# A state-space and attention kernel with a hand-written slot table: the projection of u, its copy and the softplus take earlier slots

## What is computed

```python
# layer 1
xn = layernorm(x) * (1 + scale) + shift               # from silu(c) @ ada_w
x_in, z = split(xn @ in_proj_w.T)                     # 512 channels each
u = silu(causal_conv4(x_in) + conv_b)
dt_r, B, C = split(u @ x_proj_w.T, [64, 80])          # 64 + 16 + 16 rows: "x_dbl"
dt = softplus(dt_r @ dt_proj_w.T + dt_proj_b)
h[t] = h[t-1] * exp(dt * A) + (dt * u) * B            # 512 channels x 16 states
y = (sum_n h * C + u * D) * silu(z)
x = x + gate * (y @ out_proj_w.T)
# layer 2
q, k, v = projections of layernorm(x); q = softmax over head, k = softmax over positions
y = q @ (k.T @ v);  x = x + silu(layernorm(y) * (1 + s) + t) @ W_out + b_out
```

## Time and profile before

| | us |
|---|---|
| median of 3 runs (lowest, highest) | 557.86 (556.59, 559.77) |
| the profiled execution, its own time | 559.76 |
| its span in the trace | 558.0 |
| VectorE busy | 504.7 |
| POOL, PE and ScalarE busy | 449.6, 438.2 and 430.8 |
| VectorE idle ahead of scans, for ScalarE's decays | 10.9 in 14 waits |

### The profile page before, as it was taken

How to read it: one execution, slowest core, us unless ns; L and a number is a source line. 1 busy time by engine, 2 the same in 40 slices (tenths; PEclk the granted TensorE clock), 3 DMA queues, 4 the chain that set the end, 5 groups by cost and what they waited for, 6 DMA issues and landing times. The chain is left out here.

```text
span 558.0 us, 7398 instructions
## 1 busy us (share of the span) xinstructions
PE 438.2 (79%) x2438; PEld 364.5 (65%) x2438; DVE 504.7 (90%) x520; ACT 430.8 (77%) x992; POOL 449.6 (81%) x306
## 2 busy tenths in 40 slices
PE   8968756769688788779788678769677878959797
PEld 7657445557576677657676667658565766847675
DVE  2489899999999989999999999999999988999853
ACT  2694868689879989798979989799877797686444
POOL 4059979989997989979997999979997979995121
PEclk8978868887899698998899899989899697779899
DMA  8295043102330144011430044003320044000001
GB/s 250 90 330 150 0 140 97 68 23 77 120 114 2 28 153 170 3 28 52 152 122 0 29 156 168 0 11 117 122 85 9 2 165 159 1 0 20 1 1 38
DMA packets 22366, 45.38 MB, mean 81 GB/s; under 512 B 3684, under 2 KB 13556, under 8 KB 22328
## 3 DMA queue, kind: packets, MB, share of 16 engines
q1 hardware_dynamic: 22328, 44.92, 24.6%
HBM read 42.52 MB, written 2.39 MB: 80 GB/s over the span
## 5 line engine op out<-in xcount | busy, mean ns | idle before, releaser
L545 POOL TENSOR_TENSOR hs<-dtu,Br 128x1024 f32<-128x1024 f32 x127 | 296.8, 2360 | 7.9 <-DMA Br<-bc_rows 6.9
L766 ACT ACTIVATE ring<-dt,Aneg 128x256 f32<-128x256 f32 x512 | 212.7, 464 | 44.0 <-DVE hs L1012 39.1
L1000 DVE TENSOR_TENSOR_SCAN ring<-ring,hs 128x1024 f32<-128x1024 f32 x97 | 221.6, 2284 | 10.9 <-ACT ring L766 10.9
L1370 PE MATMUL sums<-ident,hs 128*128 128x128 f32 x1024 | 154.9, 309 | 49.4 <-DVE hs L1012 49.3
L1370 PEld LDWEIGHTS sums<-ident,hs 128*128 128x128 f32 x1024 | 138.6, 162 | 60.6 <-DVE hs L1012 57.5
L1012 DVE TENSOR_TENSOR hs<-ring,Cr 128x1024 f32<-128x1024 f32 x96 | 117.5, 1224 | 3.3
L554 POOL TENSOR_TENSOR hs<-hs,Cr 128x1024 f32<-128x1024 f32 x31 | 73.0, 2356 | 38.7 <-DVE hs L1000 38.7
L1000 DVE TENSOR_TENSOR_SCAN hs<-ring,hs 128x1024 f32<-128x1024 f32 x31 | 70.3, 2268 | 0.0
L1437 PE MATMUL PY<-wqkvo,xT 128*128 128x256 f32 x168 | 48.3, 439 | 0.0
L1437 PEld LDWEIGHTS PY<-wqkvo,xT 128*128 128x128 f32 x168 | 39.6, 236 | 7.7
L1363 PE MATMUL sums<-ident,uD 128*128 128x128 f32 x64 | 14.3, 310 | 32.3 <-DVE ygT L1019 32.3
(11 more groups left out here) (232 smaller groups left out, 681.7 us busy)
## 6 DMA issues: line engine op xcount, KB each, us to landing
Br<-bc_rows SPq DMA_DIRECT2D x32, 512.0 KB, 5.3
Cr<-bc_rows SPq DMA_DIRECT2D x32, 512.0 KB, 4.0
xg<-in_x SPq DMA_DIRECT2D x8, 256.0 KB, 3.0
out<-fin SPq DMA_DIRECT2D x7, 256.0 KB, 4.3
hs<-in_ada_wT SPq DMA_DIRECT2D x3, 512.0 KB, 5.1
win<-in_in_wT SPq DMA_DIRECT2D x2, 512.0 KB, 6.9
hs<-in_W_emb SPq DMA_DIRECT2D x2, 512.0 KB
gate<-gate_rows SPq DMA_DIRECT2D x8, 128.0 KB, 3.1
```

Source lines behind the costliest of these rows:

```text
L545: nc.gpsimd.tensor_tensor(hs[:, g % DBUF], dtu[:, b % 2, dc, :].unsqueeze(1).to_broadcast([P, NQ, T]), Br[:, NQ * q:NQ * q + NQ, :], ALU.m ...
L766: ins = nc.scalar.activation(ring[:, g % 2, j, :], dt[:, b % 2, dc, :], ACT.Exp, scale=Aneg[:, c:c + 1])
L1000: V.tensor_tensor_scan(driven if by_pool(g) else decays, decays, driven, 0.0, ALU.mult, ALU.add).then_inc(s_scan_done, 1)
L1370: ins = M(YT[:, c, :], hs[:, g % DBUF, j, P * c:P * c + P], ident[:, :], is_transpose=True, start=False, stop=(q == UPC - 1 and j == NQ - ...
```

## The change

On TensorE `x_proj` goes from slot -9 behind `output` to slot -10 ahead of it, and `dt_proj_0` from slot -8 to -9. On ScalarE `copy_xdbl` goes from slot -6 to -8, `softplus_parts_0` from -5 to -6, `softplus_parts_1` from -3 to -4, and `norm1`, which keeps slot 26, now stands ahead of `softplus_parts_0` in the table. Entry 0 keeps its old place by an extra line. Slots -6 and 26 and 42 are all position 10.

```diff
                 for slot, step in (..., (-14, conv_last_tap_1),
-                                   (-11, copy_z), (-6, copy_xdbl), (-5, softplus_parts_0), (-3, softplus_parts_1),
-                                   (19, copy_yg), (25, normalize1), (26, norm1), (30, exp_q), (30, exp_k), (31, mask_v), (32, copy_qT),
+                                   (-11, copy_z), (-8, copy_xdbl), (26, norm1), (-6, softplus_parts_0), (-4, softplus_parts_1),
+                                   (19, copy_yg), (25, normalize1), (30, exp_q), (30, exp_k), (31, mask_v), (32, copy_qT),
                                    (33, copy_kT), (36, normalize2), (42, finish), (-29, moments0)):
...
+                    if step is softplus_parts_0 and g in (-6, -5):
+                        b = 0 if g == -5 else None
...
-                                   (-13, in_proj_3), (39, output), (-9, x_proj), (-8, dt_proj_0), (-6, dt_proj_1),
+                                   (-13, in_proj_3), (-10, x_proj), (39, output), (-9, dt_proj_0), (-6, dt_proj_1),
```

## The result

The changed kernel takes 569.86 us (median of 4 runs, 569.21 to 570.15), the kernel before beside it 557.25 us (4 runs, 556.59 to 559.77): a ratio of 1.0216, 95% interval 1.0181 to 1.0251. The forecast was 566.3 us, with a range of 561.8 to 573.0. Two profiles can be compared term by term: 569.21 us and a span of 567.4 after, 559.76 and 558.0 before, so 9.4 us between the spans. The rest of the 12.6 us between the medians lies between each profiled execution and its median: before, the median was 2.5 us lower, after, 0.65 us higher. In the ratios of this document runs over 1.5% above the fastest of their own kernel are left out, though not in the medians: one in "The softplus put back" and three in "x_proj alone".

A forecast was written before the change was run, and what follows sets the result against it. VectorE, 90% busy, was taken to bound the kernel, so only its idle time could change. Window losses of +5.0 and TensorE lateness of 3.4 gave +8.4 us on the 557.86 median: 566.3 us, range 561.8 to 573.0.

The forecast's parts named there:

- The bound: VectorE, 90% busy with an unchanged instruction list, bounds the kernel; the change can act only on its idle time.
- The window: ScalarE, position 10's decays to position 11's scan: 5.85 us available, 5.36 needed before the change, 7.39 after.
- The forecast's 1.54 us a window: Excess of ScalarE's work over the window, waited for by VectorE in units 43, 59, 75, 91 and 107.
- the forecast's 5.0: First sum for position 11: 7.70 us in five windows plus 1.06 in unit 27, less 3.79 of waits removed.
- TensorE's lateness: Moved x_proj delays ScalarE at TensorE's lower clock: 0.85 us in each of four entries, 3.4 in all.
- The 3.0 us through `transpose_x1` and `norm1`: In unit 43's entry at half clock, transpose_x1 ends up to 3.0 us after norm1 wants it.
- The upper bound of +15.4: TensorE lateness of 3.0 us in three entries and 1.4 in unit 27, on top of 5.0.
- What was costed at nothing: Zero cost for softplus_parts_1 between decays of positions 12 and 13, later finish, earlier broadcasts and later sums of position 7.
- a sign of being wrong: VectorE beginning to wait in a position held for covered: 8, 12 or 13.
- Its other terms at nothing: Zero taken for unit 11's decays (bounds 0 and 0.5 us) and, within the upper bound, position 8's gating product.
- The rival of a slow TensorE: TensorE stays as slow as in the profile before: +15.4 us, 573.3 us; chance 0.17.
- a TensorE fast everywhere: Filling the gap raises the clock before x_proj in all entries, only the window counts: +5.0, 562.9 us; chance 0.25.

The follow-up runs named there:

- The softplus put back: Changed kernel with both softplus halves back in slots -5 and -3, its other moves kept: 562.18 us, ratio 1.0045 to the kernel before.
- x_proj alone: Kernel before with only x_proj moved from slot -9 to -10, ahead of the sums of position 7 and output: 558.74 us, ratio 0.9978.
- the second profile: Profile of the changed kernel timed once more, unedited, beside the kernel before: 569.05 us, ratio 1.0181.

## Why the forecast was right, and where it was not

**The bound.** Right: VectorE's instruction list is unchanged and the time moved with its idle time. Of 9.4 us between the profiles, 7.5 are waits for decays (18.4 less 10.9).

**The window.** Right, and shown from four sides: 7.37 us needed for the 7.39 forecast; the wait gone with the softplus outside; 1.3 us less with 1.27 us of it outside; 0.97 us more with 0.96 us added. The forecast's 1.54 us a window came out as 1.51, 1.43 of it shown as wait. Five such windows are 7.6 us. Unit 27 adds 1.0 for 1.06: its decays and scan need 6.87 us (134.63 to 141.50 in the changed kernel) in a window of 5.85. What went away is 4.05 us, for by its steps x_proj alone is 1.65, 0.71 and 1.69 us shorter at units 43, 59 and 107, where the waits read 3.79. That makes 4.5 for the forecast's 5.0.

**TensorE's lateness.** "I take 0.85 in each of the four, 3.4" was too much: by steps it is 1.1 us in units 42 and 43 (0.85 of it the wait of 2.28 above 1.43), 0.4 in unit 27 and nothing in 59 and 107, so about 1.6 in all; in the second profile unit 91 has 0.84 too. Of the two ways to be late only the smaller came, the copy waiting for `x_proj`. The 3.0 us through `transpose_x1` and `norm1` did not, since behind a slow `x_proj` TensorE was at its upper level again (TensorE and ScalarE in the changed kernel, units 40 to 42):

```profile
192.30 3.12 PE L1325 MATMUL PX<-u,wxp 128*96 128x256 f32 x8
...
195.26 1.04 PE L1372 MATMUL sums<-ident,hs 128*128 128x128 f32 x8
195.46 0.38 ACT L696 ACTIVATE xdbl<-PX 96x256 f32<-96x256 f32 x1 [1.75 <-PE PX L1325]
...
199.81 0.60 PE L1238 MATMUL PZ<-ident,xh 128*128 128x128 f32 x4
...
200.45 1.02 ACT L793 ACTIVATE xT<-PZ,par 128x256 f32<-128x256 f32 x2
```

`transpose_x1` ends at 200.41, and `norm1` starts at 200.45. The upper bound of +15.4 rested on those 3.0 us. The granted clock in positions 7 to 10 was between 0.57 and 0.90 before and 0.75 to 0.89 after, and at its lowest, 0.75, unit 43 is late. The Trainium skill's rule of idle gaps, named in the forecast ("TensorE: Matmul & The Clock Gate", section "HAM oscillation"), is borne out in part: with `x_proj` in the gap the lowest of these stretches rose (entries 1, 2, 3 and 6 from 0.57, 0.58, 0.67 and 0.57 to 0.85, 0.75, 0.89 and 0.89). But the two others fell, from 0.89 and 0.90 to 0.83, and over the whole span the softplus put back, which has `x_proj` in the same gap, was granted 0.865 where the kernel before had 0.887.

**What was costed at nothing.** This step failed: "`softplus_parts_1` goes between the decays of positions 12 and 13; the long position 11 of VectorE covers it". In entry 0, for entry 1's softplus, position 11 isn't long, as `max_qk` has slot 27 and first runs in unit 27. The timeline of the changed kernel, TensorE and ScalarE around unit 12:

```profile
80.08 3.68 PE L1372 MATMUL sums<-ident,hs 128*128 128x128 f32 x16 [6.09 <-DVE hs L1014]
...
83.55 1.91 PE L1344 MATMUL PX<-xdbl,wdt 97*128 97x256 f32 x4
...
85.50 0.60 ACT L708 ACTIVATE dt<-PX 128x512 f32<-128x512 f32 x1 [3.77 <-PE PX L1344]
...
87.81 3.25 ACT L766 ACTIVATE ring<-dt,Aneg 128x256 f32<-128x256 f32 x8
```

ScalarE stands 3.77 us for `dt_proj_1`, which is behind 16 sums, and then the softplus of 2.3 us is ahead of the decays of unit 13. In the kernel before, those decays came first and the softplus behind them:

```profile
83.02 1.67 ACT L766 ACTIVATE ring<-dt,Aneg 128x256 f32<-128x256 f32 x4 [1.36 <-DVE hs L1012]
84.95 0.60 ACT L708 ACTIVATE dt<-PX 128x512 f32<-128x512 f32 x1 [0.26 <-PE PX L1342]
```

In the later entries ScalarE waits there too (1.75 us in unit 76), and there the cover held, as the forecast said. This wait, 2.09 to 2.22 us, is in every profile that has the move in entry 1, and in none of the three versions of the changed kernel without it. TensorE's level has a part in it: around unit 12 the granted clock is 0.50 and the 16 sums take 3.68 us, around unit 76 it is 1.00 and they take 1.91. An estimate from these rows: at 1.00 the sums and `dt_proj_1` would be through some 2.6 us sooner, more than the 2.22 us of the wait. That wasn't tried. The forecast had named such a wait in position 13 as a sign of being wrong, and in this place it was. Its other terms at nothing held in the profile: no scan of units 11 and 12 waits for decays, and no gating product of position 8 for the sums.

**The sum.** +8.4 was forecast from 5.0 and 3.4. Measured in the profile are 4.5 for the windows, 1.6 for TensorE's lateness in them (together the 6.1 of the table), 2.3 for unit 13, and 0.9 for the rest: losses of 3.2 us outside the windows, less 2.3 us that the profile before happened to lose. So the path was right and the closeness of the sum was in part luck: the two terms that it names came to 6.1 of 8.4, and the wait at unit 13, put at nothing, made up the 2.3 that were missing. In the two groups of rounds that timed both kernels the medians differ by 12.6 and 9.6 us, both more than 8.4. The rival of a slow TensorE (+15.4) did not come; that of a TensorE fast everywhere (+5.0) fell short by unit 13 and by what follows. The range, by its own rule (the fast case less one, up to the slow case), would be 561.9 to 573.3; the forecast has 561.8 to 573.0.

**What stays open.** Which level TensorE's clock has in a given entry, and so where the last 2 to 3 us fall, is not settled: runs of one kernel spread over up to 10 us, two profiles of the changed kernel differ in units 83 and 91, and filling gaps moved the losses more than it removed them. Why the order with early copy and late softplus meets the lower level in positions 0 to 3 in all five entries of its profile wasn't tried.

## What to carry to other kernels

Where a two-buffer ring couples two engines, count the window: from the release of one buffer to the next use of the other, and what the producer must do in it. Here it held 5.85 us, 5.36 were used, and 2.3 us of movable work pushed in cost their excess in each of six places, while the same work one slot later was free. And check a cover in every entry by name, the first and the last above all: a long position may be long only from the second entry on, and the engine that feeds the moved work may be at its lower clock there.

## What was not expected of the hardware

TensorE's level of 1.2 GHz costs time in this kernel although TensorE is idle for over a fifth of the span (busy 77%): a stretch of VectorE's work of 15.34 us took 17.05 where the granted clock was 0.80 (the softplus put back). The same program's runs spread from 554.75 to 562.06 us, and a change that removes 4 us of waits in one profile ("x_proj alone") could not be told from none by its runs (0.9978, 0.9937 to 1.0019).
